# One-core graph, mix and expert layer: folded mix matrices, centred key weights, split one-hot matrices and three-quad rings in the edge stage

## The reference, cut to what matters

```python
xn = _layernorm(x)                          # x is 6250 x 256
x = x + gnn(xn, src, dst, edge_weight) + mix(xn[None])[0]
x = x + ffn(_layernorm(x)[None])[0]

def gnn(x, rows, cols, edge_vals):          # 100000 edges, dst sorted
    new_x = segment_sum(edge_vals[:, None] * x[cols], rows)
    out1 = tanh(batchnorm(new_x @ hamilton1) * gamma + beta)
    return out1 @ hamilton2

def mix(x):                                 # 8 heads of 32
    q, k, v = split(x @ w_qkv + b_qkv)      # per head
    kv = einsum('bhnd,bhne->bhde', _ln(k), _ln(v)) / HW
    ret = einsum('bhnd,bhde->bhne', q, kv) + x
    return gelu(ret @ w1 + b1) @ w2 + b2 + x
```

## Time and profile before

| what | value |
|---|---|
| median of 3 runs | 2387.26 us |
| profiled execution, whole | 2384.72 us |
| its span, first to last instruction | 2383.3 us |
| PE / DVE / ACT / POOL busy in the span | 1934.3 / 1713.1 / 1128.4 / 1278.8 us |
| mean granted TensorE clock | 0.891 |
| first and last put start | 108.4 us, 1352.2 us |

### The profile page before, as it was taken

One profiled execution on the slowest core, in us unless ns is written; L12 is line 12 of the kernel. 1 busy time (PEld: TensorE's weight loads), 2 busy tenths in 40 slices (PEclk: granted clock), 3 DMA queues, 4 the chain that ended last, 5 costly groups with the idle time before them and its releaser, 6 DMA issues. The chain is left out here.

```text
span 2383.3 us, 38273 instructions
## 1 busy us (share of the span) xinstructions
PE 1934.3 (81%) x11227; PEld 1607.3 (67%) x11251; DVE 1713.1 (72%) x5437; ACT 1128.4 (47%) x2236; POOL 1278.8 (54%) x811
## 2 busy tenths in 40 slices
PE   2559997697888878887877266985899999999995
PEld 1437775565665656656666134872799999999995
DVE  4848898687767858673333076888788888988884
ACT  1324443222232332323222114236899999999993
POOL 1447787578778877766777600000355444455542
PEclk8579998799998989888999598665899999999997
DMA  7878877477787787868888673223588888878885
GB/s 232 283 189 153 168 115 126 76 127 121 122 156 132 125 163 134 177 98 192 176 171 165 97 223 112 68 89 107 150 232 233 234 232 233 232 233 234 233 233 167
DMA packets 325710, 401.93 MB, mean 169 GB/s; under 512 B 34841, under 2 KB 267054, under 8 KB 325364
## 3 DMA queue, kind: packets, MB, share of 16 engines
q1 hardware_dynamic: 193822, 256.71, 34.9%
q0 software_dynamic: 103008, 103.83, 32.2%
q10 hardware_dynamic: 28662, 38.84, 5.3%
HBM read 251.12 MB, written 154.55 MB: 170 GB/s over the span
## 5 line engine op out<-in xcount | busy, mean ns | idle before, releaser
L1094 POOL DMA_INDIRECT acc_dram<-third x566 | 914.6, 1616 | 343.0 <-issue 138.6
L2016 POOL DMA_INDIRECT sum_dram<-node,small x112 | 198.2, 1770 | 316.4 <-DVE node L1945 222.7
L1873 PE MATMUL bank<-up_parts 128*128 128x256 f32 x2688 | 334.4, 284 | 2.3 <-DVE up_parts L1903 2.3
L1886 PE MATMUL bank<-down_parts 128*128 128x256 f32 x2688 | 335.4, 284 | 0.0
L1873 PEld LDWEIGHTS bank<-up_parts 128*128 128x128 f32 x2688 | 329.2, 193 | 2.7 <-DVE up_parts L1903 2.7
L1886 PEld LDWEIGHTS bank<-down_parts 128*128 128x128 f32 x2688 | 325.3, 191 | 0.0
L551 PE MATMUL bank<-work,third 128*128 128x256 f32 x1132 | 294.4, 403 | 27.8 <-ACT third L1049 27.7
L1049 ACT ACTIVATE third<-bank 128x512 f32<-128x512 f32 x283 | 168.6, 597 | 290.1 <-DMA acc_dram<-third 234.5
L857 DVE TENSOR_SCALAR third<-fixed,third 128x128 f32<-128x128 f32 x566 | 164.2, 369 | 161.0 <-PE bank L540 142.0
L1998 POOL DMA_INDIRECT node<-xh_dram,small x112 | 135.5, 1209 | 242.2 <-DVE small L1699 208.4
L551 PEld LDWEIGHTS bank<-work,third 128*128 128x128 f32 x1132 | 217.9, 205 | 63.9 <-ACT third L1049 31.6
(11 more groups left out here) (268 smaller groups left out, 3237.4 us busy)
## 6 DMA issues: line engine op xcount, KB each, us to landing
turned<-in_w_up SPq DMA_DIRECT2D x56, 1024.0 KB
turned<-in_w_down SPq DMA_DIRECT2D x56, 1024.0 KB
work<-src_dram SPq DMA_DIRECT2D x141, 256.0 KB
acc_dram<-fixed SPq DMA_DIRECT2D x15, 1280.0 KB, 13.2
work<-xn_dram SPq DMA_DIRECT2D x146, 128.0 KB
work<-acc_dram SPq DMA_DIRECT2D x72, 256.0 KB, 3.5
at_dram<-turned ACTq DMA_DIRECT2D x48, 256.0 KB
work<-at_dram ACTq DMA_DIRECT2D x24, 512.0 KB, 4.5
```

What stands on the lines that cost most here:

```text
L1094: e.indirect_dma_start(acc_dram[i], bass.IndirectOffsetOnAxis(put_i[:, t:t + 1], 0), M[:, t % (2 * QUAD), :], None, compute_op=ALU.add).th ...
L1873: k = e.matmul(ps, W1s[:, 2 * b + wp, q, h * P:(h + 1) * P], xTs[:, 2 * b + xp, q, :], start=(q == 0 and (wp, xp) == TERMS[0]), stop=(q == ...
L1886: k = e.matmul(bank[5 + c][:, 0:D], hTs[:, hp, h, c * P:(c + 1) * P], W2s[:, 2 * b + wp, h, :], start=(h == 0 and hp == 0 and wp == 0), st ...
L2016: e.indirect_dma_start(sum_dram, bass.IndirectOffsetOnAxis(slot_i[:, n:n + 1], 0), yb[:, i % 2, c, :], None, compute_op=ALU.add).then_inc( ...
```

## The change

The queries are no longer computed. From KV, the query weights (transposed on the host, `WqT`) and the first mix layer `Wm1` the kernel builds once `Wm1 + Wq KV Wm1` and the matching bias, in place (four steps behind the keys), so a chunk needs two layers instead of four products. The keys' and values' weights and bias are centred per head once (`centre`), which replaces the sum and the subtraction for each tile; ScalarE squares straight from PSUM, and a column of ones beside the values gives one of the two column sums. In the dense part VectorE writes one_lo as two fp32r halves (the rounded weight and its remainder) in one instruction of 256 columns, ScalarE makes one_hi by Abs and Relu in two, TensorE takes two fp32r products, and ScalarE clears A in 13 pieces while it is being transposed. The first group is 6 wide instead of 5. M, OH and the loads of the stored matrices get rings of three. The row number of a put is a maximum instead of a sum. The costs are new, so that keys take quads 2 to 41 (before 1 to 31), the dense part 45 to 113 (before 32 to 112), the products 114 to 137 (before 113 to 137).

```diff
-DENSE = ((0, 108, 5), (108, 152, 6), (152, 188, 6), (188, 216, 7))
+DENSE = ((0, 108, 6), (108, 152, 6), (152, 188, 6), (188, 216, 7))
+ROW_QUADS = 3
-        OH = third(2 * QUAD, P)
+        OH = third(S_QUADS * QUAD, P)
-        M = third(2 * QUAD, D)
+        M = third(ROW_QUADS * QUAD, D)
-        dense_cost = [2.0, 0.5, 0.5]
+        dense_cost = [0.6, 0.6, 0.6]
-            dense_cost += [0.8] * (b - a + 2) + [0.7] * (-(-HI // 4) + 1)
+            dense_cost += [0.25] * (b - a + 3) + [0.2] * (-(-HI // 4) + 1)
-        costs = [2.0] + [2.8] * (NT + 4) + [1.0] * 2 + cost_in_turn + [2.4] * (2 * PRODUCTS)
+        costs = [0.6] * 3 + [0.9] * NT + [0.4] * 4 + [0.5] * 4 + cost_in_turn + [0.53] * (2 * PRODUCTS)
...
+            e.wait_ge(s_kvready, 1)
+            for g in range(2):
+                e.matmul(bank[6 + g][:, 0:D], KV[:, g, :], WqT[:, g, :], start=True, stop=False)
...
+                    k = e.matmul(bank[6 + m][:, 0:D], folded[:, g, m * P:(m + 1) * P], Wm1[:, g, :], start=(g == 0), stop=(g == 1))
...
-                    t = a + i - 1
+                    t = a + i - 2
...
+                        e.wait_ge(s_away, HOT_DONE[t])
+                        for i_ in range(2):
+                            k = e.matmul(dense_bank(n)[:, 0:even(HI * s)], one_lo[:, t % 4, i_, :], one_hi[:, t % 3, 0:even(HI * s)],
+                                         start=(i_ == 0), stop=(i_ == 1))
...
-                    e.tensor_reduce(ksum, rows, AX.X, ALU.add).then_inc(s_kvln, 1)
...
-                    e.scalar_tensor_tensor(out=d3, in0=spread16(ksum), scalar=-1.0 / HD, in1=rows,
-                                           op0=ALU.mult, op1=ALU.add).then_inc(s_kvln, 1)
...
-                        e.tensor_scalar(one_lo[:, t % 4, :], iota_p, lo_col[:, t:t + 1], w_c[:, t:t + 1], ALU.is_equal, ALU.mult)
-                        e.tensor_scalar(one_hi[:, t % 3, 0:HI * s], iota_n[:, 0:HI * s], hi_col[:, t:t + 1], None,
-                                        ALU.is_equal).then_inc(s_one, 1)
+                        e.scalar_tensor_tensor(out=one_lo[:, t % 4], in0=iota_p.unsqueeze(1).broadcast_to((P, 2, P)),
+                                               scalar=lo_col[:, t:t + 1], in1=parts_w[:, t, :].unsqueeze(2).broadcast_to((P, 2, P)),
+                                               op0=ALU.is_equal, op1=ALU.mult).then_inc(s_one, 1)
...
-                    e.memset(A, 0.0).then_inc(s_clear, 1)
...
+                        e.activation(away[:, t % 2, 0:even(HI * s)], iota_n[:, 0:even(HI * s)], ACT.Abs, bias=far_col[:, t:t + 1]).then_inc(s_away, 1)
...
+                        e.activation(one_hi[:, t % 3, 0:even(HI * s)], away[:, t % 2, 0:even(HI * s)], ACT.Relu, bias=ones[:, 0:1],
+                                     scale=-1.0).then_inc(s_away, 1)
...
-                    if q >= 2:
-                        for u in (t - 2 * QUAD, t + 1 - 2 * QUAD):
+                    if q >= ROW_QUADS:
+                        for u in (t - ROW_QUADS * QUAD, t + 1 - ROW_QUADS * QUAD):
```

More of the change, by code:

```diff
@@ L68, in gps_layer, with even @@
     HI = NT
+    def even(n):
+        return n + n % 2
+    LINE = even(HI * WIDEST)
     NQ = -(-(ET - T0) // QUAD)
```

450 lines of the change are left out of this document (238 added, 212 removed).

## The result

The changed kernel takes 2424.64 us, the median of 4 runs (2416.32 to 2433.93), against 2386.06 for the kernel before in the same comparison: ratio 1.0164, 95% interval 1.0123 to 1.0204. It is slower by 1.6%, where 2319 us was forecast, and it lies outside the range. The profiled execution took 2416.32 us with a span of 2414.8.

What follows compares the result with a forecast made beforehand. The prediction took the pace of 566 puts as the bound, held in the dense part by a VectorE-PE loop: 174 + 300 + 44 + 547 + 178 + 41 = 1284 us for the last put, so 2319 us, range 2275 to 2366.

Steps and rivals of the forecast that it cites:

- Keys: Key stretch: the puts bound it, between 7.46 and 8.4 us a quad, taken as 7.9 for 38 quads, 300 us.
- The cover over the fold and tables: Between keys and dense part: three ready quads last 22.4 us against the gap, so 8.8 us a quad for 5 quads.
- Puts beside clearings: Dense group ends: clearings move from VectorE to ScalarE, saving up to 5.8 us each, with no put of 7 us left.
- Start: First sixteen puts, to 174 us: left as they are, cost 0, or 4 us if the cover is thin.
- The stages behind the last put: Code after the last put, some 1031 us: untouched by the change and carried over, wrong if differing by more than 5 us.
- the dense part's loop: Dense part: loop of VectorE's select, dense tiles and PE's products takes 8.05 us a quad, 547 us for 68 quads.
- The sum's form: Dense part: select, tiles, quad's products and hand-overs added in series, 8.4 us before the change where 8.32 was measured.
- The pair: ScalarE, dense part: Abs and Relu of 294 columns at 503 ns each, 1.0 us a tile without overlap.
- C: Rival, chance 0.08: ScalarE's in-order queue becomes the dense part's bound, 2430 us, or 2400 at 1.4 us a pair.
- A: Rival, chance 0.20: landings set every quad after the start at 8.4 us, with three puts in flight; 2355 us.
- B: Rival, chance 0.09: three ready quads in the ring hide the loop, puts run at 7.7 us a quad; 2259 us.
- D: Rival, chance 0.06: the loop lengthens through higher density as it shortens, and the fold eats the rest; 2387 us.

Runs made afterwards that it cites:

- e3: Changed kernel with the ring of M back at two quads instead of three: 2439.80 us.
- e13: Changed kernel, split kept, with VectorE's select and indices moved between its two halves of a quad's steps: 2340.45 us.
- e16: Changed kernel with VectorE's select between its halves of steps, but TensorE and ScalarE taking all steps behind combine: 2402.99 us.
- e6: Changed kernel with key cost 0.5 and product cost 0.4, so 3.2 dense tiles a quad: 2332.66 us, ratio 0.9742 to the kernel before.
- e14: Changed kernel with select between the halves of steps and costs giving 3.2 dense tiles a quad: 2317.04 us, ratio 0.9709 to the kernel before.
- e9: Changed kernel with all of a quad's steps unsplit, ahead of between and combine: 2349.61 us.
- e10: Changed kernel with all of a quad's steps unsplit, behind combine: 2342.54 us.
- e12: Kernel before the change with all of a quad's steps ahead of between and combine: 2369.88 us, ratio 0.9911.
- e1: Changed kernel with one_hi made by VectorE in one comparison instead of ScalarE's Abs and Relu: 2433.26 us.
- e7: Changed kernel with one_hi made by VectorE and lower key and product costs, about 3.5 dense tiles a quad: 2360.75 us.
- e4: Changed kernel with four small bf16 filler products on TensorE ahead of each dense tile's products: 2431.94 us.

## Why the prediction was wrong

**What held.** Keys: 7.9 us a quad foretold, 7.99 measured, with PE at 83% of 174 to 462 us. The cover over the fold and tables: 8.8 foretold for five quads, 8.33 measured, and no gap over 5 us there; e3 shows that the third quad of M helps to hide them. Puts beside clearings: gone. Start: 174.2 before and 174.4 now. The stages behind the last put: 0.7 us apart. From 174 to 514 us 344 was summed and 340 taken; from 1160 to the last put 219 was summed (178 + 41) and 224 taken. (The first of these sums held 43 quads for 42, so for each quad it was 0.1 us low.)

**The step that failed** is one, the dense part's loop: "8.05 us x 68 quads = 547 us". It took 646 us, 9.5 a quad, and these 99 us are all but 1 of the 100 by which the last put missed 1284.

*What the sum left out.* It did set select behind `between` and `combine`, one after the other, but with one dense tile on each side. Four tiles a quad stood beside it only as work ("VectorE's own work is 2.76 + 4 x 0.73 + 0.3 = 6.0, not a bound"), so of the density I asked only whether an engine is full. What the density changed is how many tiles lie between VectorE's interruption (at the end of a quad's steps) and TensorE's (in their middle): two at 4.0 tiles a quad, fewer at 3.25. In the timeline the second tile behind `combine` waits for ScalarE's second copy and a pair, 1.98 us where the sum had hand-overs of 0.5, and VectorE's next select waits for that tile.

The runs give the price of the misplacement at each density: at 4.0 tiles 9.50 - 8.37 = 1.13 us a quad (changed kernel, e13), with the sign turned 9.22 - 8.37 = 0.85 (e16), and at 3.1 tiles 8.08 - 7.99 = 0.09 (e6, e14), within the scatter. For 68 quads 1.13 us are 77; by e9 (8.42) and e10 (8.33) it would be 73 and 80. Why it costs so little at 3.1 tiles is not separated: fewer tiles lie between the two, and there the puts themselves hold a quad near 8.0, so that a longer loop could hide behind them. That VectorE and TensorE can run only a few tiles apart (one_lo has four places, one_hi three, and there are two banks) is my reading of why the places matter, and no run tests it.

*The agreement that was luck.* The sum's form gave 8.4 for a measured 8.32, "which is why I trust this form". But in e12 most of select lies beside `between` and `combine` (69%, for 31% before), so they no longer stand in series, and the dense quad still takes 8.35; there ScalarE waits 101.6 us for landings between 514 and 1100 us, before 34.5. So the series was at best one of two limits of about the same length before the change, and one match at that point could not tell whether its form was right.

*What is left.* With the interruptions side by side the quad takes 8.37, not 8.05: 0.32 us, 22 us in all. This is no longer the loop that was summed, so it can't be laid on single terms. What the rows show is that VectorE's tile is 0.95 us where 0.73 was summed, since one_lo is 0.48 and the sum 0.47, for 0.35 and 0.38. The pair itself was foretold well. In the dense part, by form:

```profile
L1001 ACT ACTIVATE work<-fixed,turned 128x294 f32<-128x294 f32 x185 | 99.4, 539 | 4.3 <-issue 0.2
L1007 ACT ACTIVATE hots<-work,ones 128x294 fp32r<-128x294 f32 x186 | 97.7, 526 | 0.0
...
L781 DVE TENSOR_TENSOR turned<-turned,bank 128x294 f32 x187 | 88.1, 471 | 171.1 <-PE bank L506 148.3 <-issue 20.4 <-DVE turned L781 0.9
```

503 ns were expected, 539 and 526 measured, and a pair repeats every 1.0 us. The estimate of 525 ns for 294 columns, from the Trainium skill's formula in "ScalarE: Activation LUTs", section "What ACT_TABLE_LOAD costs", is the better of the two here; it would not have changed the sum.

**The rivals.** C was the one on the side that came, and its times (2400 to 2430) hold the result, but its mechanism is refuted. ScalarE was busy 59% of the dense part, where its sign of being right was over 85%; with ScalarE's pairs gone the kernel is no faster (e1), and at the lower density the same (e7); and in e13 all pairs are there, TensorE waits for them as long as before, and the quad takes 8.37. Its quad of 9.5 at c = 1.4 is the measured one, for another reason, and over 68 quads where it had 54. The rule in the Trainium skill's "ScalarE: Activation LUTs", section "Rules for kernel authors", gives VectorE's advantage for each element in bf16. Here the data are fp32 and VectorE's instruction is a comparison; it takes 0.39 us against two of 0.53 on ScalarE, so the direction agrees, and it is worth nothing in time. A, the landings, is no part of the loss (84.7 us of POOL's waits, before 84.5), and its price of 8.4 us a quad is refuted by the 7.99 of the keys and of e14's dense part. B fell with the result itself: with three quads in the ring the dense quad takes 9.50, with two 9.58 (e3). D had the right words, "the loop lengthens through the higher density as it shortens", but gave them 6 in 100 and 2387 us, 38 too few.

**Slips in the sums.** None decides anything. The chance of faster, 0.57 + 0.20 + 0.09 and half of 0.06, is 0.89 and not 0.87. ScalarE's quad with 525 ns for each of its eight instructions is 6.8 at most, not 6.7. The low end of the forecast's own range comes to 2284, not 2290.

**The clock.** From 514 to 1100 us it fell from 0.92 before to 0.85. Row of the kernel before, to be held against those under e4:

```profile
514.00:1100.00 586.00, 487.60 (x2130) 355.84 (x2128) 416.21 (x1664) 180.28 (x305) 454.11 (x278) 0.92 0.78 140
```

e4 raised the clock and gained nothing, but paid for it with PE's time; e13 gained 84 us and the clock rose with it, to 0.90. The products of `combine` over the same stretch, changed kernel and then e13:

```profile
L575 PE MATMUL bank<-work,third 128*128 128x256 f32 x496 | 145.3, 445 | 0.0
```

```profile
L575 PE MATMUL bank<-work,third 128*128 128x256 f32 x560 | 145.3, 405 | 0.0
```

Those of `between` took 334 and 311 ns. Eight of each stand in a quad, so some 0.5 us of the 1.13 (an estimate from these means: 8 x 0.040 + 8 x 0.023) can be the clock on TensorE's interruption. It came and went with select's place, so the clock is a part of the price and not a second cause; how much of the 1.13 would stay at an equal clock is open.

**What was not tried.** More banks or a longer ring for one_lo, so that the two engines may run further apart, would test the same cause from the other side.

## What to carry to other kernels

When two in-order engines work a common list of steps and each interrupts it for work of its own, put both interruptions at the same step of the list: then they overlap, otherwise they can add up. Before raising the number of steps for each round, count the steps between the two interruptions, not only each engine's busy time; a split into halves that cost nothing measurable at three steps cost an eighth of the round at four. And when a model of a loop agrees with one measurement, change the one thing that the model says is the bound before trusting it: the unsplit order of e12 would have shown that the series was not the only limit.

## What was not expected of the hardware

The price of a misplacement is steep: 0.09 us a quad at 3.1 tiles (e6, e14) and 1.13 at 4.0 (e13), though part of that may be the puts' own pace at the lower density. Raising the granted clock from 0.85 to 0.93 by filler (e4) moved two puts of 249. And taking ScalarE's work from 359 to 162 us in 586 (e1) gained nothing at all, with VectorE's going from 367 to 418: busy time did not tell which engine to relieve.
